# The recurrent part of a GRU block: TensorE's steps 64 to 495 as loops, side products from scaled 16-bit parts

## What is computed

```
def cell(h, x):                        # 512 steps one after the other, for 4 batches at once
    gi = x @ W_ih + b_ih               # the input's gates: 512 -> 1536
    gh = h @ W_hh + b_hh               # the state's gates: 512 -> 1536
    r = sigmoid(i_r + h_r); z = sigmoid(i_z + h_z)
    n = tanh(i_n + r * h_n)
    return (1 - z) * n + z * h
x = x + scan(cell, cond, x)            # "x3" in the kernel
x = x + L3(x, cond)                    # out[b] = x3[b] @ (identity + interpolation matrix of cond[b])
```

## Time and profile before

| | |
|---|---|
| median of 3 runs | 2287.54 us (2285.54 to 2287.59) |
| profiled execution | 2289.45 us, its span 2287.7 us |
| mean granted TensorE clock | 0.969 of full speed |
| busy share of the span | PE 95%, PEld 80%, DVE 67%, ACT 56%, POOL 21% |
| instructions in the span | 130256, of them 56269 matmuls and as many weight loads |

### The profile page before, as it was taken

One profiled execution on the slowest core, in us unless ns is written; L12 is line 12 of the kernel. 1 busy time (PEld: TensorE's weight loads), 2 busy tenths in 40 slices (PEclk: granted clock), 3 DMA queues, 4 the chain that ended last, 5 costly groups with the idle time before them and its releaser, 6 DMA issues.

```text
span 2287.7 us, 130256 instructions
## 1 busy us (share of the span) xinstructions
PE 2174.7 (95%) x56269; PEld 1832.3 (80%) x56269; DVE 1531.9 (67%) x6093; ACT 1279.5 (56%) x5574; POOL 486.7 (21%) x2271
## 2 busy tenths in 40 slices
PE   5768999999989999999999999999999999999998
PEld 3654655545545999999999999999999999999997
DVE  7987978869687456666666566666556566656665
ACT  6765947759467455566445455544445454544444
POOL 2002121021211122222222222222222222222222
PEclk8569999999999999999999999999999999999999
DMA  5000000010010000000000000000000000000000
GB/s 204 3 2 1 1 1 1 1 56 1 1 56 1 22 5 5 5 5 5 5 5 10 5 9 9 5 10 5 9 9 5 9 5 10 10 5 14 12 9 16
DMA packets 8710, 31.47 MB, mean 14 GB/s; under 512 B 1028, under 2 KB 1352, under 8 KB 7880
## 3 DMA queue, kind: packets, MB, share of 16 engines
q1 hardware_dynamic: 7712, 23.07, 2.7%
q10 hardware_dynamic: 424, 0.07, 0.0%
HBM read 18.94 MB, written 4.19 MB: 10 GB/s over the span
## 4 chain that ended last, share of the span: by engine, by line
PE 81%; DVE 12%; ACT 4%; issue 2%; DMA 1%; POOL 0%; SPq 0%; POOLq 0%; ACTq 0%; DVEq 0%
PE psum L1923 53%; PE psum L1830 9%; PE psum L1733 3%; PE psum L1654 3%; PE psum L1696 2%; PE psum L1751 2%; PE psum L1857 2%; PE psum L1717 2%; DVE region_cols L1102 2%; DVE region_cols L1086 2%; DVE top L1279 2%; ACT region_rows L750 1%; PE psum L1673 1%; DMA region_cols<-in_L_cond_W_emb_dram 1%; PE psum L1870 1%
## 5 line engine op out<-in xcount | busy, mean ns | idle before, releaser
L563 POOL TENSOR_TENSOR region_w_b<-region_w_b 128x16 f32<-128x16 f32 x1022 | 224.2, 219 | 1154.9 <-DVE region_w_b L1488 1154.9
L1923 PE MATMUL psum<-parts0A,region_w_hh 128*128 128x40 f16 x12288 | 429.5, 179 | 3.0 <-ACT psum L819 0.9
L1923 PE MATMUL psum<-parts1A,region_w_hh 128*128 128x40 f16 x12288 | 429.9, 179 | 2.4 <-issue 0.6
L1923 PE MATMUL psum<-parts1B,region_w_hh 128*128 128x40 f16 x12288 | 429.5, 179 | 2.0 <-issue 1.8
L1923 PE MATMUL psum<-parts0B,region_w_hh 128*128 128x40 f16 x12288 | 428.8, 179 | 0.4 <-issue 0.2
L1923 PEld LDWEIGHTS psum<-parts0A,region_w_hh 128*128 128x128 f16 x12288 | 381.2, 96 | 40.8 <-DVE parts0A L1497 4.4
L1923 PEld LDWEIGHTS psum<-parts1A,region_w_hh 128*128 128x128 f16 x12288 | 381.4, 96 | 40.5 <-DVE parts1A L1497 5.0
L915 ACT ACTIVATE mixA<-rzA 128x8 f32<-128x8 f32 x512 | 110.7, 216 | 535.6 <-DVE rzA L1462 535.6
L1923 PEld LDWEIGHTS psum<-parts1B,region_w_hh 128*128 128x128 f16 x12288 | 363.6, 96 | 4.8 <-issue 3.0
L1923 PEld LDWEIGHTS psum<-parts0B,region_w_hh 128*128 128x128 f16 x12288 | 363.4, 95 | 2.6 <-issue 0.4
L1462 DVE TENSOR_REDUCE rzA<-psum 128x8 f32<-128x32 f32 x512 | 98.4, 192 | 279.2 <-PE psum L1923 278.8
(11 more groups left out here) (243 smaller groups left out, 3316.2 us busy)
## 6 DMA issues: line engine op xcount, KB each, us to landing
region_rows<-in_x_dram SPq DMA_DIRECT2D x4, 1024.0 KB, 11.5
region_w_a<-in_L_cond_W_qkv_dram SPq DMA_DIRECT2D x1, 3072.0 KB, 23.4
region_w_hh<-in_L_cond_W_hh_dram SPq DMA_DIRECT2D x4, 768.0 KB, 6.6
region_w_a<-in_L_cond_W_ih_dram SPq DMA_DIRECT2D x1, 3072.0 KB, 10.3
out_dram<-region_w_b SPq DMA_DIRECT2D x12, 256.0 KB, 2.3
region_cond<-in_cond_dram SPq DMA_DIRECT2D x2, 1024.0 KB, 8.1
region_cols<-in_L_cond_W_emb_dram SPq DMA_DIRECT2D x1, 2048.0 KB, 19.8
region_w_out<-in_L_cond_W_out_dram SPq DMA_DIRECT2D x1, 1024.0 KB, 21.5
```

The costliest lines, as they stand in the source:

```text
L563: e.tensor_tensor(k.line[half][:, :, :, 1:3], new.unsqueeze(3).broadcast_to([P, 2, B, 2]), k.signs.unsqueeze(1).unsqueeze(1).broadcast_to( ...
L1923: made = e.matmul(k.slots(bank)[:, :, ch, :, 0:2], k.w16[:, 2 * read + c, part, NC * "rzn".index(g) + 2 * half + ch], k.parts[now][read][: ...
```

## The change

1. **Loops.** PE's steps 64 to 495 are no longer unrolled. Fifteen loop nests, one step in the innermost body, take their place: seven for the gates of chunks 3 to 8 and the free steps 112 to 127 (`pe_gate_loop`, `pe_free_loop`), eight for the rows (`pe_row_loop`). Each begins at an instruction address that is a multiple of 256. The step number is a register, and so are the values waited for and the addresses of the side product.
2. **Side products** in the loops are four 16-bit matmuls of 256 columns in place of one 32-bit one. W_ih, x, x3 and the sampling matrix are scaled by powers of two and split into a 16-bit high part and the 16-bit rest; all four products of parts are made. All write with `start=False` to a bank that ACT has filled with zeros (`act_clear`), so that every body is the same. The semaphore counts products, `NC` = 4 for a group.
3. **Making the parts** is new work at the end of steps: DVE takes maxima (steps 0 to 27, 512 elements each), ACT makes high parts (256 or 512 elements), DVE the rests (256 elements), one DVE item in a step. The scaled results are unscaled as ACT takes them.
4. **Sums stay in PSUM.** `rz` and `nline` are views of the banks that the sums are read from (`HELD`), so DVE writes and ACT reads PSUM there.
5. **`parts` has one buffer** per half. DVE's `partsA` now also waits for `readA`, which PE sends after unit `ABn`. PE's waits for `zsum` and `nline` go.
6. Steps 496 to 511 and the last products use 16-bit parts too, unrolled.

```diff
-        self.parts = [[small(f"parts{parity}{half}", 2, B, 2, dtype=FP16) for half in "AB"] for parity in range(2)]
-        self.rz = [small(f"rz{h}", 2, 2, B) for h in "AB"]
+        self.parts = [small(f"parts{half}", 2, B, 2, dtype=FP16) for half in "AB"]
+        self.rz = [[self.bank(banks[half], 2, B, at=HELD) for banks in (R_BANK, Z_BANK)] for half in range(2)]
-        self.nline = [small(f"nline{h}", 2, B, 4) for h in "AB"]
+        self.nline = [self.bank(i, 2, B, 4, at=HELD) for i in N_BANK]
...
+def act_clear(e, k, n):
...
+    e.activation(k.bank(SIDE_BANK[n % 2], HALF_ROW), k.zero[:].broadcast_to([P, HALF_ROW]), ACT.Copy).then_inc(s["cleared"], 1)
...
+def act_input_high(e, k, q, c):
...
+    e.activation(k.x_parts[:, q % 2, c, 0], k.xT[:, c, :, STARTS[q]:STARTS[q] + LONG], ACT.Copy,
+                 scale=k.in_scale[:, 1:2]).then_inc(s["x_halved"], 1)
...
+def dve_input_low(e, k, q, c):
...
+    e.scalar_tensor_tensor(k.x_parts[:, q % 2, c, 1], k.xT[:, c, :, STARTS[q]:STARTS[q] + LONG], k.in_scale[:, 1:2],
+                           k.x_parts[:, q % 2, c, 0], ALU.mult, ALU.subtract).then_inc(s["x_lowered"], 1)
...
-def dve_parts(e, k, half, st, nxt):
+def dve_parts(e, k, st, half):
...
     e.wait_ge(s[f"line{h}"], st + 1)
+    if half == 0:
+        e.wait_ge(s["readA"], st + 1)
...
+    for st in range(LOOPED):
+        pe_step(e, k, st)
+        pe_side(e, k, st)
+    for q in range(2, CHUNKS):
+        at = STARTS[q]
+        if q + 1 < CHUNKS:
+            pe_gate_loop(e, k, q + 1)
+            at += 12 * NC
+        if q == 2:
+            pe_free_loop(e, k, at, STARTS[3])
+        else:
+            tile, second = divmod(q - 3, 2)
+            pe_row_loop(e, k, at, B * tile + 2 * second)
+    for second in range(2):
+        pe_row_loop(e, k, LATE_PRODUCTS + 4 * NC * second, B * (NT - 1) + 2 * second)
+    for st in range(NEXT_PRODUCTS, S):
+        pe_step(e, k, st)
+        pe_side(e, k, st)
...
+def pe_gate_loop(e, k, q):
...
+    e.addr_align(PE_BLOCK, max_nops=4)
+    with e.Fori(0, 6) as pair:
+        with e.Fori(0, 2) as parity:
+            with e.Fori(0, NC) as c:
+                turn = pair * (2 * NC) + parity * NC + c
+                pe_step(e, k, turn + first)
+                e.wait_ge(s["cleared"], pair * 2 + parity + (done // NC + 1))
...
+                pe_looped_products(e, k, w_parts, turn * (2 * P), x_parts, c * (2 * B * LONG) + q % 2 * 2 * NC * B * LONG,
+                                   B * LONG, parity)
...
+def pe_looped_products(e, k, stationary, at, moving, moving_at, moving_part, parity):
+    s = k.sem
+    to = k.psum.rearrange("p b n -> p (b n)")[:, bass.ds(parity * 512 + SIDE_BANK[0] * 512, HALF_ROW)]
+    for low in range(2):
+        for part in range(2):
+            made = e.matmul(to, stationary[:, bass.ds(at + low * P, P)], moving[:, bass.ds(moving_at + part * moving_part, HALF_ROW)],
+                            start=False, stop=True, skip_group_check=True)
+    made.then_inc(s["side_products"], 1)
```

More of the change, by code:

```diff
@@ L140 @@
 SIDE = side_table()
-BANK_USE = [("gates", 0, j) for j in range(12)] + [group for _, groups, _ in side_plan() for group in groups]
 def side_done(s):
     return [(group, number % 2) for group, number, part in SIDE.get(s, ()) if part[-1] == NC - 1]
-FREE = [st for st in range(2 * LONG) if st >= LONG and not side_done(st)]
-PLACE_STEPS = {st: i for i, st in enumerate(range(44, 44 + 3 * B))}
-HAT_STEPS = {st: i for i, st in enumerate(FREE[:2 * B * NC])}
-def add_table():
[L156 to L165, removed]
+FIRST_HALVED = 3
@@ new lines, in act_x3_high @@
+def act_x3_high(e, k, u):
+    s = k.sem
+    tile, b = divmod(u, B)
+    if tile == NT - 1:
+        e.wait_ge(s["x3"], TILE_SUMS + NC * (b // 2 + 1))
+    else:
+        e.wait_ge(s["x3"], NC * (u + 1))
+    if tile:
+        last = [n for n, (kind, _, *args) in enumerate(LOOP_GROUPS) if kind == "rows" and args[0] == ROW_GROUPS * (u - B) + 1][0]
+        e.wait_ge(s["side_products"], NC * (last + 1))
+    e.activation(k.x3_parts[:, b, :, 0], k.xT[:, :, b, x3_columns(tile)], ACT.Copy, scale=k.in_scale[:, 1:2]).then_inc(s["x3_halved"], 1)
@@ L1426, in dve_gru @@
         first = k.state[:, 0, 2 * half:2 * half + 2]
-        e.tensor_copy(k.parts[0][half][:, :, :, 1], first).then_inc(done, 1)
+        e.tensor_copy(k.parts[half][:, :, :, 1], first).then_inc(done, 1)
         e.tensor_copy(k.line[half][:, :, :, 2], first).then_inc(done, 1)
@@ L1514, in pe_program @@
     pe_gru(e, k)
-    rows = slice(*LAST)
     for part in range(ROW_GROUPS):
@@ new lines, in pe_step @@
+def pe_step(e, k, st):
+    s = k.sem
+    first_step = isinstance(st, int) and st == 0
+    for u in GRU_UNITS:
+        read, h, g = "AB".index(u[0]), u[1], u[2]
+        half = "AB".index(h)
+        bank = {"r": R_BANK, "z": Z_BANK, "n": N_BANK}[g][half]
+        if u in ("AAr", "BAr"):
+            if first_step:
+                e.wait_ge(s["gru_first"], 18)
+                e.wait_ge(s["w_kept"], NC)
+                e.wait_ge(s["w_low"], NC)
+            else:
+                e.wait_ge(s[f"low{u[0]}"], st)
+        if u in ("AAr", "ABr"):
+            e.wait_ge(s[f"put{h}"], st + 1)
+        for ch in range(2):
+            for c in range(2):
+                for part in range(2):
+                    made = e.matmul(k.slots(bank)[:, :, ch, :, 0:2], k.w16[:, 2 * read + c, part, NC * "rzn".index(g) + 2 * half + ch],
+                                    k.parts[read][:, c].unsqueeze(1).broadcast_to([P, COPIES, B, 2]),
+                                    start=read == ch == c == part == 0, stop=(read == 1), skip_group_check=True)
+        if LAST_OF[g, h] == u:
+            made.then_inc(s[f"{g}_products{h}"], 1)
+        elif u == "ABn":
+            made.then_inc(s["readA"], 1)
@@ L1939, in build, with pe_side @@
+def pe_side(e, k, st):
+    for (kind, *args), number, products in SIDE.get(st, ()):
+        if kind == "gates":
+            pe_gate_products(e, k, *args, products, number)
+        else:
+            pe_next_products(e, k, *args, products, number)
 def build(nc, *args):
```

469 lines of the change are left out of this document (324 added, 145 removed).

## The result

The changed kernel takes 2590.01 us (median of 4 runs, 2587.40 to 2593.41) against 2287.57 us of the kernel before on the same chip: a ratio of 1.133, with a 95% interval of 1.1316 to 1.1346. It is 13% slower. The forecast was 2258 us, the range ended at 2325. The profiled execution took 2593.41 us, its span 2591.7.

A forecast was written before the change was run, and what follows sets the result against it. PE was taken to bound side-product steps, the recurrence standing only 0.09 us below. From 2289.45 us, -33 - 16 + 13 + 3 + 3 + 1 = -29 gave 2260 profiled, 2258 us median; range 2238 to 2325.

The forecast's parts named there:

- Control on PE: PE's sequencer between steps: nine instructions at 51 ns, 0.46 us, hidden under a cover of 0.67 us.
- The outer loops: Extra branches of PE's outer loops, with late bodies and thin margins: 0.03 us a step, +13 us (0 to +43).
- Rival 1: PE's sequencer between steps: control not hidden, 1.3 us, 0.6 over cover, +260 us; chance 0.24 for 2292 to 2450 us.
- Side products: PE's four 16-bit matmuls of 256 columns take 0.44 instead of 0.52 us a step, -33 us over 416 steps.
- Half A's wait: PE's wait before loading half A, now on a sequencer addition: just fits, load at 1502.10, new products ending at 1502.22.
- Instruction fetch: PE's loop bodies, if fetched once, remove the 17.6 us of stalls: -16 us taken (0 to -17.6).
- half B's: PE's wait before loading half B: load at 1502.98 at the earliest, PE there at 1503.02, fits by 0.04 us.
- Rivals 3 and 4: Every branch refetches the body: 2500 us up, chance 0.03; loops gain nothing on fetch: 2274 us, 0.18 shared with Rival 2.
- Sums in PSUM: DVE's writes and ACT's reads of the sums in PSUM: +0.02 us (-0.09 to +0.10), taken as zero.
- Rival 2: Recurrence-bound through PSUM sums: steps of 2.89 instead of 2.84 us, 2272 us; chance 0.18 shared with loops gaining nothing on fetch.
- New work: Making parts on DVE and ACT: DVE +3 us (0 to +10), ACT 0, maxima of steps 0 to 27 0.
- The tail: After the last step DVE splits four more pieces, +1.5 us; steps 496 to 511 save 0.5.

The follow-up runs named there:

- e5_flat: e4_early with its three nested loops written as one flat loop whose counter gives part and bank; 2278.10 us against 2279.98 of the kernel before, ratio 0.9994.
- e9_spread: e5_flat with the input scale's maximum taken from POOL, and smaller register programs spread behind nine products; 2249.45 us against 2285.80 of the kernel before, ratio 0.9843.
- e4_early: Changed kernel with the five register programs moved inside the step instead of between its last product and the side products; 2325.36 us, ratio 1.0191 to the kernel before.
- e1_unrolled: Changed kernel with PE's loops written out step by step, no register programs or branches; 2291.75 us against 2281.49 of the kernel before, ratio 1.0045.
- e8_sbuf: e5_flat with DVE's sums of r, z and n back in SBUF; 2277.10 us in one run.
- e2_fixed: Changed kernel with side-product inputs at fixed addresses, only the bank and the wait's value from registers; 2372.37 us in one run.
- e7_twolate: e5_flat with two register programs put back between the step's last product and the side products; 2290.26 us in one run.

## Why the prediction was wrong

**Control on PE** is the step that failed: "Nine instructions at 51 ns are 0.46 us. That fits". There are nine, but they take 0.79 us, not 0.46, because register programs take 51 to 153 ns and a taken branch 208; and the sum left out the 0.06 to 0.11 us between two of them, 0.58 us in all. The cover was put at 0.67 us and is 0.8. So some 0.54 us are exposed in a regular gate step and 0.78 in a row step, not nothing. That row steps have one program more and longer ones was left out altogether. I had asked for the cost of one instruction and never for that of going to the next, though the threshold had been named and the sum stood only 0.2 us below it. The Trainium skill, "Advanced Engine Details and Errata", section "Control Flow Timing", gives 108 ns for a compare-and-branch; the taken ones here take 208. That alone would not have turned the forecast: 208 ns and eight times 51 are 0.62 us, still under 0.67. The longer programs and the gaps did.

**The outer loops** were in the +13 us. At a nest's end branch, move, branch and head program follow each other: in the changed kernel every fourth step pays 0.42 us on top and every eighth 0.84, which is (0.42 + 0.84) / 8 = 0.16 us for each step. `e5_flat` took it away. From the changed kernel's stretch to that of `e9_spread` it is 1565.1 - 1231.1 = 334 us for all control, where I had 13. Of these 209 lie in the 288 gate steps and 125 in the 128 row steps.

**Rival 1** had the mechanism and the place, with 0.24 of the chance. Its 1.3 us of control are right partly by luck: 0.4 of them stood for eight register addresses, which cost nothing (`e4_early`), and 0.9 for the nine instructions, which take 1.31 to 1.37. Its +260 us must be held against the 334, and even its stretch of times, up to 2450 us, ends below the 2590 measured. What spoke for it, that the wait of `lowA` takes away all lead, was worth more than the one row of 51 ns against it. The range was closed where it let exposed control be 0.15 us over the cover.

**Side products** were right: 0.44 us in `e1_unrolled` and `e4_early`, their starts 108 to 109 ns apart, as by the formula that the prediction quotes, and steps of 2.84 us, the floor that the prediction gives. **Half A's wait** fits as worked out, and as narrowly: in `e9_spread` the next 96 begin 0.11 us after the end of the addition that waits for half A, and 0.06 is the least seen. Of half B's nothing shows. **Instruction fetch** was right as well: packets fell from 333 to 15, and where 17.6 us stood above the sum of regular steps, 3.9 are left in `e9_spread` (1231.05 - 1227.1), about what its loops' last steps add, for which the prediction had +3. Side products and fetch together were put at -49 us, and its stretch is 46.6 us shorter than that of before. What the prediction did not see is how much the loops are needed. Written out, the faster steps lose 44 us (`e1_unrolled`), and the change as a whole is 0.45% slower than the kernel before. Rivals 3 and 4 are refuted by this and by the packets.

**Sums in PSUM:** the zero stands for steps with a side product; PE binds them. Free steps gained 0.03. ACT's activation fell from 216 to 185 ns, and DVE's sums rose by 7 to 13 ns (half A's from 192 to 200 and 221 to 229), not by the 52 that the prediction took from other operations. Rival 2 did not happen (and its +0.03 us a step did not follow from its own 2.89 against 2.84).

**New work:** that of DVE and ACT in the loops costs nothing that shows. "The maxima of steps 0 to 27 [...] 0" holds for the maxima, 675 ns each, but I had not priced the reduction on POOL that follows them: +10.7 us. The trace of before had its price, at the two reductions over the partitions there, the idle time ahead at one and the idle time behind at the other (timeline of POOL):

```profile
37.76 0.37 POOL L448 PARTITION_ALL_REDUCE absmax<-most  x1 [5.57 <-issue]
...
596.02 0.38 POOL L452 PARTITION_ALL_REDUCE hh_absmax<-hh_chunk_most  x1 [15.01 <-DVE hh_chunk_most L1032]
603.19 1.26 POOL L500 TENSOR_TENSOR region_work<-region_work,gain 128x512 f32<-128x512 f32 x1 [6.79 <-issue]
```

**The tail** was put at +1.0 and is +5.1 us. The last products are one part of it: 64 matmuls of the 32-bit form took 3.71 us, the 128 of 16-bit parts 5.37, and ahead of them stand ACT's and DVE's splitting of the last piece, 0.41 and 0.36. The chains of before and of the changed kernel:

```profile
2280.15 3.71 PE psum L1522 x64
```

```profile
2581.56 0.41 ACT region_cond L1003
2581.97 0.03 issue
2581.99 0.36 DVE region_cond L1633
2582.35 0.04 issue
2582.40 5.37 PE psum L1791 x128
```

The other 2.6 us lie in steps 496 to 511, some of which take 3.1 to 3.7 us. The chain has pieces of issue there, as in the earlier trace rows:

```profile
2537.89 0.53 issue
```

The work of these steps is not what is slow, since in `e8_sbuf` they take 44.5 us, 0.15 more than before. Late instructions, where written-out code begins again, would fit. That is not shown, and the cause stays open.

## What to carry to other kernels

A loop on an engine that feeds a recurrence is free only while its control fits under the work that is queued ahead; count every sequencer instruction with its gap (here 0.15 us each on average, in the changed kernel's gate steps), and put address programs into the body, away from waits that empty the queue. Flatten nests, since each level's end is paid in one piece. And before an engine that sits in a recurrence is given another kind of instruction, look in the trace at what it did around the last one of that kind.

## What the runs showed of the hardware

- PE's sequencer, by these traces: a register program 41 to 225 ns, more with its length and above all with remainders and quotients; an addition 32 to 50; a move 29 to 40; a compare-and-branch 207 to 211 taken for the most part, in some places over 300, and 67 to 79 not taken; from the end of one to the start of the next 0.06 to 0.11 us where nothing is waited for.
- The lead of the sequencer was 16 products: the first late program started 0.41 us ahead of the last of the 96 in the changed kernel, in `e2_fixed` and in `e7_twolate`, in gate loops and row loops alike.
- A matmul with its addresses in registers costs no more than one with fixed addresses: four take 0.44 us in both forms. With register programs between them they took 0.50 to 0.53.
- POOL stood still for 5.5 to 6.1 us ahead of a reduction over the partitions and 6.7 to 7.6 behind it, wherever in these traces it waited for nothing else. In the changed kernel the one at 856.05 us is the third, so this is not paid once only. The Trainium skill, "GPSIMD Engine Reference", section "2.1 Instruction dispatch", has the first part (approximately 6 us for the first call of a freshly loaded kernel), and these traces agree. The way back costs as much again.
- PE's written-out code lost 17.6 us in 432 steps of 2.92 us and 44 us in steps of 2.84 with nearly the same packets (333 and 339).
